# First expert layer of a two-layer perceiver block: tokens moved by indirect DMA, weights asked for one by one, shared expert placed under the scatter

## What is computed

```python
shared = jax.nn.silu(xf @ sg) * (xf @ su) @ sd
masked = expert_scores * group_mask + (1.0 - group_mask) * -1000000000.0
top_scores, top_idx = jax.lax.top_k(masked, K)          # K = 4 of E = 32
gates = jax.nn.softmax(top_scores, axis=-1)
capacity = max(1, int(N / E * K * CAP_FACTOR))          # 80
...
pos = jnp.cumsum(onehot, axis=0)[jnp.arange(N * K), flat_e] - 1
keep = pos < capacity
buf = jnp.zeros((E + 1, capacity, d), xf.dtype).at[e_s, p_s].set(xf[tok])[:E]
h = jax.nn.silu(jnp.einsum('ecd,edh->ech', buf, wg)) * jnp.einsum('ecd,edh->ech', buf, wu)
out_e = jnp.einsum('ech,ehd->ecd', h, wd)
gathered = out_e[flat_e, jnp.minimum(pos, capacity - 1)]
contrib = gathered * (flat_g * keep.astype(xf.dtype))[:, None]
routed = jnp.zeros_like(xf).at[tok].add(contrib)
return (shared + routed).reshape(b, s, d)
```

## Time and profile before

| | us |
|---|---|
| median of 3 timed runs | 2116.39 (2115.75 to 2123.99) |
| profiled execution | 2112.91 |
| its span | 2110.3 |
| routing of layer 0's experts, to the first gather's one-hot | 1029.5 to 1067.4 |
| its 32 experts | 1067.4 to 1364.9 |
| granted TensorE clock, mean over the span | 0.926 of 2.4 GHz |

### The profile page before, as it was taken

How to read it: one execution, slowest core, us unless ns; L and a number is a source line. 1 busy time by engine, 2 the same in 40 slices (tenths; PEclk the granted TensorE clock), 3 DMA queues, 4 the chain that set the end, 5 groups by cost and what they waited for, 6 DMA issues and landing times. The chain is left out here.

```text
span 2110.3 us, 38732 instructions
## 1 busy us (share of the span) xinstructions
PE 1838.4 (87%) x12992; PEld 1069.2 (51%) x12992; DVE 1165.8 (55%) x2102; ACT 865.3 (41%) x1653; POOL 178.9 (8%) x335
## 2 busy tenths in 40 slices
PE   8999799999999627578699999869999999829588
PEld 4444334444444314338489999824444444416587
DVE  5777578888888336365211101158888888427311
ACT  2222146666667303125121111127666667503222
POOL 2212110000000000001000000010000000000000
PEclk9999979999999859889699999969999999869699
DMA  6596664444442260000368665334434343082042
GB/s 192 182 228 181 172 93 61 60 60 60 60 60 31 97 84 0 0 1 1 121 140 263 220 225 175 100 55 62 60 59 58 58 59 55 1 92 80 20 161 70
DMA packets 147896, 198.09 MB, mean 94 GB/s; under 512 B 24696, under 2 KB 121736, under 8 KB 141592
## 3 DMA queue, kind: packets, MB, share of 16 engines
q1 hardware_dynamic: 145756, 195.24, 41.3%
q10 hardware_dynamic: 2064, 1.87, 0.3%
HBM read 158.16 MB, written 38.92 MB: 93 GB/s over the span
## 5 line engine op out<-in xcount | busy, mean ns | idle before, releaser
L1079 ACT ACTIVATE probs<-ps 128x512 f32<-128x512 f32 x1024 | 573.9, 595 | 287.9 <-PE ps L1006 276.4
L1091 DVE TENSOR_REDUCE top<-ps 128x1 f32<-128x1024 f32 x512 | 601.1, 1220 | 36.0 <-PE ps L987 33.6
L987 PE MATMUL ps<-kst,qst 105*128 105x512 bf16 x1024 | 318.8, 394 | 36.3 <-POOL qst L945 28.3
L1006 PE MATMUL ps<-qst,kst 105*128 105x256 bf16 x2048 | 344.4, 275 | 2.3 <-DVE qst L1103 1.8
L1020 PE MATMUL ps_o<-probs,vst 128*32 128x256 f32 x4096 | 328.5, 392 | 0.8 <-ACT probs L1079 0.8
L1006 PEld LDWEIGHTS ps<-qst,kst 105*128 105x128 bf16 x2048 | 176.3, 100 | 215.2 <-ACT probs L1079 72.1
L987 PEld LDWEIGHTS ps<-kst,qst 105*128 105x128 bf16 x1024 | 65.9, 98 | 190.3 <-DVE top L1091 90.5
L2039 DVE TENSOR_TENSOR hT<-silu,ps_h 128x320 f32<-128x320 f32 x32 | 15.6, 488 | 264.0 <-ACT silu L2000 264.0
L1020 PEld LDWEIGHTS ps_o<-probs,vst 128*32 128x32 f32 x4096 | 80.7, 108 | 109.9 <-issue 89.9
L477 PE MATMUL ps_k<-ctxT,wk 128*128 128x512 f32 x256 | 122.2, 600 | 1.0 <-DVE square_weights L642 1.0
L1963 PEld LDWEIGHTS ps_h<-xe,wgu 128*128 128x128 f32 x1024 | 119.2, 192 | 4.2 <-DMA wgu<-in_L_ffn_wu_dram 1.2
(11 more groups left out here) (318 smaller groups left out, 2160.7 us busy)
## 6 DMA issues: line engine op xcount, KB each, us to landing
kst<-kd SPq DMA_DIRECT2D x384, 128.0 KB
kd<-kp SPq DMA_DIRECT2D x64, 384.0 KB, 2.6
wgu<-in_L_ffn_wg_dram SPq DMA_DIRECT2D x32, 512.0 KB, 3.7
wgu<-in_L_ffn_wu_dram SPq DMA_DIRECT2D x32, 512.0 KB, 4.6
wd<-in_L_ffn_wd_dram SPq DMA_DIRECT2D x32, 512.0 KB, 3.8
w<-in_L_ffn_w_dram SPq DMA_DIRECT2D x16, 1024.0 KB, 5.5
ctx_sb<-in_ctx_dram SPq DMA_DIRECT2D x16, 512.0 KB, 5.8
vd<-square_weights SPq DMA_DIRECT2D x16, 512.0 KB, 4.1
```

What stands on the lines that cost most here:

```text
L987: mm = pe.matmul(ps1[:, u % 2, x * 512:(x + 1) * 512], qst[:, m, qt * P:(qt + 1) * P], kst[:, m, c * W1 + x * 512:c * W1 + (x + 1) * 512], ...
L1006: mm = pe.matmul(ps2[:, u % 2, x, :], kst[:, m, kt * P:(kt + 1) * P], qst[:, m, :], start=True, stop=True)
L1079: nc.scalar.activation(probs[:, u % SLOTS, :, :], ps2[:, u % 2, :, :], ACT.Exp).then_inc(probs_ready, 1)
L1091: v.tensor_reduce(top[:, b, u // NC1, u % NC1:u % NC1 + 1], ps1[:, u % 2, :], AX, ALU.max).then_inc(mx, 1)
```

## The change

Routing and experts become one stage. VectorE turns the place of a token in each of its four experts into a row number of a table in HBM with 80 rows an expert (row; a dropped token gets a number out of bounds, which a transfer skips). GpSimd scatters xn into that table with 16 indirect transfers of 128 rows (4 token tiles x 4 choices). SyncE brings each expert's 80 rows back into one of eight buffers xr, TensorE turns them (`turn`), ScalarE copies them into xe. The output ye of each expert is stored to a second table. When all are stored, GpSimd gathers the rows with 16 indirect transfers into back, and VectorE adds them, each times its share, to what the shared expert and the residual gave. disp, comb, combT, the gathers and the combinations on TensorE are gone. The first table is cleared once, by a transfer of 2.6 MB at the start of layer 0's cross attention.

ps_h has two buffers, and TensorE runs the first layer of e+1 before the second layer of e. SyncE asks for wgu of e+3 after the first layer of e+1, for wd of e+2 after the second layer of e, then for the rows of e+8, and then stores ye of e. All four stacks of keys and five parts of the values are asked for right after the first two experts' weights; three parts follow near the end of the loop and eight after it. The shared expert is moved behind the selection, on all engines. The auxiliary query rows are asked for at the start of `pieces_to_dram`, and qall is opened after the experts. The loop holds eight experts instead of two.

```diff
+def zero_expert_rows(pr, sp):
+
+    nothing = pr.inp["kaux"][0, 3:5, :].bitcast(F32).rearrange("r (x d) -> (r x) d", d=D)
+    n = nothing.shape[0]
+    sp.dma_start(pr.xed.rearrange("(g r) d -> g r d", r=n), bc(nothing, 0, E0 * CAP0 // n)).then_inc(
+        pr.rows_zeroed, 16)
...
+def experts0(pr, xn, xT, residual, dst, next_cross):
 
 
     nc, inp = pr.nc, pr.inp
     R = G0 + E0
-    gate = pr.sb(st, "gate", [P, NT, E0])
-    slot = pr.sb(st, "slot", [P, NT, E0])
-    with ExitStack() as s2:
-        sb = lambda name, shape, dt=F32: pr.sb(s2, name, shape, dt)
+    NROWS = E0 * CAP0
+    SKIP = 1e6
+    XB = 8
+    VSOON, VLATE = 5, 8
+    xed, zeroed = pr.xed, pr.rows_zeroed
+    yed = nc.dram_tensor("expert_rows_out", [NROWS, D], F32, kind="Internal").ap()
...
+        xr = sb("xr", [CAP0, XB, D])
...
+        acc = pr.ps(st, "acc", [P, NT, D])
+        ps_h = pr.ps(st, "ps_h", [P, 2, 2, 512])
+        ps_x = pr.ps(st, "ps_x", [P, 2, 512])
+        ps_y = acc[:, 0:NT:2, :]
...
+        def experts(eng, body):
+
+            for e in range(XB):
+                body(e, e, {0: "first", 1: "second"}.get(e, ""))
+            with eng.Fori(1, E0 // XB - 1) as i:
+                for x in range(XB):
+                    body(XB * i + x, x, "")
+            for x in range(XB):
+                body(E0 - XB + x, x, {XB - 2: "last but one", XB - 1: "last"}.get(x, ""))
...
+                def load_gu(e):
+                    for i, name in enumerate(("L0_ffn_wg", "L0_ffn_wu")):
+                        sp.dma_start(wgu[:, e % 2, i, :, :], inp[name][e].rearrange("(c p) f -> p c f", p=P)).then_inc(
+                            gu_in[e % 2], 16)
+
+                def load_d(e):
+                    sp.dma_start(wd[:, e % 2, :, :], inp["L0_ffn_wd"][e].rearrange("(c p) f -> p c f", p=P)).then_inc(
+                        d_in[e % 2], 16)
+
+                def load_x(e):
+                    sp.dma_start(xr[:, e % XB, :], xed[e * CAP0:(e + 1) * CAP0, :]).then_inc(x_in[e % XB], 16)
...
+                for e in range(2):
+                    load_gu(e)
+                    load_d(e)
+                for m in range(NBUF):
+                    next_cross.load_constant_rows(sp, m)
+                    next_cross.load_k(sp, m // B, m)
+                for part in range(VSOON):
+                    next_cross.load_v(sp, part)
+                sp.wait_ge(scattered, 16 * NT * TOPK)
+                for e in range(XB):
+                    load_x(e)
+                sp.wait_ge(h_made, 1)
+                load_gu(2)
+                for e in range(E0):
+                    if e + 3 < E0:
+                        sp.wait_ge(h_made, e + 2)
+                        load_gu(e + 3)
+                    if e + 2 < E0:
+                        sp.wait_ge(y_made, e + 1)
+                        load_d(e + 2)
+                    if e + XB < E0:
+                        load_x(e + XB)
+                    elif VSOON <= e + XB - E0 + VSOON < VLATE:
+                        next_cross.load_v(sp, e + XB - E0 + VSOON)
+                    sp.wait_ge(y_copied, e + 1)
+                    sp.dma_start(yed[e * CAP0:(e + 1) * CAP0, :], ye[:, e % 2, :]).then_inc(y_out[e % 2], 16)
+                for part in range(VLATE, VPARTS):
+                    next_cross.load_v(sp, part)
+
+            @block.gpsimd
+            def _(pool):
+                pool.wait_ge(zeroed, 16)
+                pool.wait_ge(row_ready, 1)
                 for t in range(NT):
+                    for k in range(TOPK):
+                        nc.gpsimd.indirect_dma_start(
+                            xed, bass.IndirectOffsetOnAxis(row[:, t, k:k + 1], 0), xn[:, t, :], None,
+                            bounds_check=NROWS - 1, oob_is_err=False).then_inc(scattered, 16)
+                pool.wait_ge(sh_added, 1)
+                nc.gpsimd.memset(back[:, :, :, :], 0.0).then_inc(back_zeroed, 1)
+                pool.wait_ge(back_zeroed, 1)
+                for b in range(2):
+                    pool.wait_ge(y_out[b], 16 * E0 // 2)
+                for t in range(NT):
+                    for k in range(TOPK):
+                        nc.gpsimd.indirect_dma_start(
+                            back[:, t, k, :], None, yed, bass.IndirectOffsetOnAxis(row[:, t, k:k + 1], 0),
+                            bounds_check=NROWS - 1, oob_is_err=False).then_inc(came_back[t], 16)
...
+                pe.wait_ge(sel_ready, 1)
+                for t in range(NT):
+                    for u in range(t + 1):
+                        mm = pe.matmul(ps_n[:, t, :], pr.cb("earlier") if u == t else pr.cb("ones"), selb[:, u, :],
+                                       start=(u == 0), stop=(u == t))
+                mm.then_inc(placed, 1)
...
+                mm.then_inc(sh_added, 1)
+
+                def turn(e, x, first=False):
+
+                    b = x % 2
+                    pe.wait_ge(x_in[x], 16 // XB * (e - x) + 16)
+                    if not first:
+                        pe.wait_ge(x_copied, e - 1)
+                    for c in range(C):
+                        mm = pe.transpose(xview[:, b, c, :], xr[:, x, c * P:(c + 1) * P], pr.cf("ident")[0:CAP0, 0:CAP0])
+                    mm.then_inc(x_turned, 1)
+
+                def up(e, b, first=False):
+                    pe.wait_ge(x_copied, e + 1)
+                    pe.wait_ge(gu_in[b], 16 * (e - b) + 32)
+                    if not first:
+                        pe.wait_ge(h_done, e - 1)
+                    for i in range(2):
+                        for f in range(FT0):
+                            for c in range(C):
+                                mm = pe.matmul(hview[:, b, i, f, :], wgu[:, b, i, c, f * P:(f + 1) * P], xe[:, b, c, :],
+                                               start=(c == 0), stop=(c == C - 1))
+                    mm.then_inc(h_made, 1)
+
+                def down(e, b, first=False):
+                    pe.wait_ge(h_done, e + 1)
+                    pe.wait_ge(d_in[b], 8 * (e - b) + 16)
+                    if first:
+                        pe.wait_ge(base_ready, 1)
+                    else:
+                        pe.wait_ge(y_copied, e - 1)
+                    for f in range(FT0):
+                        mm = pe.matmul(ps_y[0:CAP0, b, :], hT[:, b, f, :], wd[:, b, f, :],
+                                       start=(f == 0), stop=(f == FT0 - 1))
+                    mm.then_inc(y_made, 1)
+
+                def expert(e, x, place):
+                    b = x % 2
+                    if not place.startswith("last"):
+                        turn(e + 2, (x + 2) % XB)
+                    if place != "last":
+                        up(e + 1, 1 - b, first=(place == "first"))
+                    down(e, b, first=(place in ("first", "second")))
+
+                turn(0, 0, True)
+                turn(1, 1, True)
+                up(0, 0, True)
+                experts(pe, expert)
...
+                def copy_x(e, b, first=False):
+                    act.wait_ge(x_turned, e + 1)
+                    if not first:
+                        act.wait_ge(h_made, e - 1)
+                    nc.scalar.copy(xe[:, b, :, :], xview[:, b, :, :]).then_inc(x_copied, 1)
+
+                def gate_half(e, b, first=False):
+                    act.wait_ge(h_made, e + 1)
+                    if not first:
+                        act.wait_ge(h_done, e - 1)
+                    nc.scalar.activation(silu[:, b, :, :], hview[:, b, 0, :, :], ACT.Silu).then_inc(silu_done, 1)
+
+                def expert(e, x, place):
+                    b = x % 2
+                    if not place.startswith("last"):
+                        copy_x(e + 2, b)
+                    if place != "last":
+                        gate_half(e + 1, 1 - b, first=(place == "first"))
+                    act.wait_ge(y_made, e + 1)
+                    if place not in ("first", "second"):
+                        act.wait_ge(y_out[b], 8 * (e - b))
+                    nc.scalar.copy(ye[:, b, :], ps_y[0:CAP0, b, :]).then_inc(y_copied, 1)
+
+                copy_x(0, 0, True)
+                copy_x(1, 1, True)
+                gate_half(0, 0, True)
+                experts(act, expert)
...
-                shared_hidden(0)
...
-                shared_hidden(1)
...
+                for t in range(NT):
+                    last = v.max(dtop[:, t, :], dest[:, t, :])
+                link(last)
+                link(v.tensor_scalar(skip[:, :, :], dtop[:, :, 0:TOPK], 0.0, SKIP, ALU.is_equal, ALU.mult))
+                v.scalar_tensor_tensor(out=row[:, :, :], in0=skip[:, :, :], scalar=-1.0, in1=dtop[:, :, 0:TOPK],
+                                       op0=ALU.add, op1=ALU.add).then_inc(row_ready, 1)
...
+                for f in range(FT0):
+                    shared_hidden(f)
+                dve.wait_ge(sh_added, 1)
+                v.tensor_tensor(dst[:, :, :], acc[:, :, :], residual[:, :, :], ALU.add).then_inc(base_ready, 1)
```

(6 more changed lines are left out.)

289 lines of the change are left out of this document (80 added, 209 removed).

## The result

The changed kernel takes 2041.63 us (median; 2038.50 to 2046.65) against 2116.07 for the kernel before on the same chip: ratio 0.9648, with a 95% interval of 0.9609 to 0.9686. That is 74.4 us less; forecast were 66 and a time of 2050. The profiled execution has a span of 2036.7 us, 73.6 less than before. The total came out close, but several of its terms were wrong and partly made up for each other: the head was 8.6 us too dear in the forecast and the waiting in the loop 3.8, the clock 3.6 too cheap.

What follows compares the result with a forecast made beforehand. TensorE was taken to bound the experts' loop: 117.0 gained, less 5 waiting, 17.1 head, 4 clock and 24.8 tail, gives 66 us. From 2112.9 profiled that leaves 2046.9, or 2050 us as timed median; range 2022 to 2088.

Steps and rivals of the forecast that it cites:

- The loop: Experts' loop: gathering, turning and combining leave TensorE, two transposes come; period 9.21 to 5.48 us, 117.0 us gained.
- Waiting in the loop: Experts' loop: TensorE waits 0.15 us an expert for weights, 5 us lost, ends 0 and 32 us.
- rival 2: Experts' loop becomes bound by DMA at about 6.5 us a period: 2077 us; chance 0.2 together with stacks holding up prefetches.
- The head: Before the first expert: first layer starts at 1087.5 us against 1070.38, a loss of 17.1 us.
- The DMA queue is later than both: Head: stacks, values and scatters empty the queue at 1086 us, after the scattered rows (1080.3) and the shared expert (1076.1).
- The clock: Start of the loop: TensorE idles over ten us, its clock falls to 1.2 GHz, another 4 us lost.
- The tail: After the last expert: landing stores, 16 gathers and last adds take 28.1 us where 3.3 stood, 24.8 us lost.
- c = 1.3 us: Head and tail: cost of one indexed GpSimd transfer, taken near the middle between 0.37 and 2.5 us.
- (1): Head and tail: index transfers go one at a time, 2.5 us each, giving 2081 us; chance 0.12.
- (3): Head and tail: index transfers over 3.6 us each make the kernel slower than before, 2161 us at 5 us; chance 0.04.
- Rival (4): Early key stacks hold the queue beyond first rows and prefetches: another 27 us, 2077; chance 0.2 together with a DMA-bound loop.
- Edits at nothing: Outside the loop: clearing the row table, moving the auxiliary query rows and making qall later were priced at nothing.

Runs made afterwards that it cites:

- e4: The changed kernel with eleven of sixteen value parts asked for beside experts 4 to 14, one each, not at the loop's end and behind it: 2047.1 us, one run.
- e10: The changed kernel with seven unread products added, six behind the shared expert and one between turns and first layer: 2041.1 us, ratio 0.9640 to the kernel before.
- e3: The changed kernel with the four key stacks and five value parts asked for behind the first eight row transfers instead of before: 2066.0 us, one run.
- e5: The changed kernel with the shared expert put back between the steps of the selection: 2048.5 us, ratio 0.9706 to the kernel before.
- e6: The changed kernel with four row buffers instead of eight, and so a loop of four experts: 2053.8 us, ratio 0.9716 to the kernel before.

## Why the prediction was right, and where it was not

**The loop, 117.0 gained.** Right in mechanism and size. The period is 5.44 us where 5.48 was worked out, TensorE is still the bound (158.87 of 160 us), and the silu and the product of the hidden parts are hidden behind the next first layer.

**Waiting in the loop, 5.** Mis-sized: 117.0 - 7.6 (clock) - 108.2 leaves 1.2 us in the profile of after, of which 0.9 show as idle time. But three profiles of one kernel had 0.9, 3.0 and 3.5 us of idle time and loops 184.3 to 189.0 long, so 5 is within what this kernel does. The upper end of 32 us (rival 2) rested on a reading of the DMA share that e4 refutes: 4.7 us of engine time an expert, not 5.5. The 7.4 us between asking and wanting leave out the third expert, which has 5.6; e10 waited there.

**The head, 17.1.** Here a step failed: "The DMA queue is later than both". The queue was put together from stacks, values and scatters, 40 us, and they took some 30, so that GpSimd's chain came last. Two prices were too dear: the stacks, 126 GB/s where 182 was measured at their start, and the scatters, 2.10 MB where the trace records 1.08. The 126 came from a subtraction in one window of the earlier trace rows, in which parts of the values were asked for too (the first at 1115.47); e3 shows that the stacks can be as slow as that, so the price was possible and did not hold here. The rest of the head's working held: row numbers at 23.0 against 24.0 us into the stage, 1.3 us a scatter, rows asked for after 46.6 against 47.3, the first rows turned and copied 49.0 against 50.8. The sentence "It would be 10 at the GpSimd's own pace" was the case that came, at 8.5.

**The clock, 4.** The mechanism was named, the term was mis-sized: 7.6 us (e10). The forecast took the seven us after the idle of the earlier trace rows at half speed; here 16 us ran at the lower level. Two first layers and a second lay in these 16 us, and nearly half of them was lost. The error hid 3.6 of the 8.6 us by which the head was too dear; that they offset each other is luck.

**The tail, 24.8.** Right, step by step: 27.2 us to the end of the last add, where 28.1 was worked out, with 1.30 us a gather. The value c = 1.3 us was a choice in a range from 0.37 to 2.5 that no row narrowed; that it measured 1.28 for a scatter and 1.30 for a gather is luck, and both the head's 8.5 and the tail's 24.2 hang on it. So rivals (1) and (3) fell: index transfers overlap. The step from one to the next is 1.30 us although the last scatter is seen as landed 1.96 us after its instruction ended (1.1 to 3.65 in the other runs), so the fixed part of a transfer is not paid again by the next. The rule weighed in the prediction (the Trainium skill, "DMA: Bandwidth & Descriptors", section "Anatomy of one DMA — SWDGE (gpsimd) path", 2.0 us and the bytes) may hold for one transfer, but transfers in a row don't add up by it: 15 steps at an estimated 2.3 us would be 34.5 us where 20.4 were measured.

**Rival (4)**, stacks that hold up the first prefetches, did not come in the order that the kernel has, and is real in another: e3 paid 22.5 us for it in its one run.

**Edits at nothing.** Clearing the table and moving the auxiliary rows: behind the stage nothing changed by over 0.1 us. Before it the time is 1.9 us longer; unchanged copies of the kernel began the stage between 1031.4 and 1037.8 us, and e5, which is the same up to there, at 1026.4, so this isn't told from drift.

So of 8.4 us by which the forecast was too small, 8.6 are the head, 3.8 the loop's waiting and 0.6 the tail, less 3.6 of clock and 1.9 before the stage; the sum of these is 7.5 (the profile's 73.6 against 66), and the rest is between profile and median.

## What to carry to other kernels

A rate that one window shows is a price for that window: the same stacks of keys ran at 182 GB/s and at under 150, each time with the DMA engines full. Give such a term a range, and bound it from below by its bytes at the full rate. When work goes from TensorE to indirect transfers, the stage gets a head and a tail in which GpSimd's pace (here 1.3 us for 128 rows of 1 KB) is the bound: put independent work over the head, order the tail so that its first transfers need only the early results, and keep TensorE busy up to the first product of the loop. In a loop bound by TensorE a short wait can cost more than itself: in e6 1.47 us of it made a period 5.2 us longer, because the clock fell behind it. A move such as the shared expert's is worth a gain or a loss of 7 us depending on whether something lies above it, so try it with its cover, not alone.
